# Reordering the start of a polynomial-interaction kernel: x on one queue, c1 ahead of D, low weights last

## What is computed

```python
for Wk, bk in zip(Ws, bs):
    z = jnp.einsum('bid,bjd->bdij', base, curr)
    curr = jnp.einsum('bdij,ijh->bhd', z, Wk) + bk[None, :, None]
    logit.append(curr)
pooled = jnp.sum(jnp.concatenate(logit, axis=1), axis=-1)
out = pooled @ lin_w + lin_b
```

## Time and profile before

| | us |
|---|---|
| median of 3 executions | 181.17 (180.68 to 181.23) |
| profiled execution, its own time | 181.1 |
| its span | 179.3 |
| TensorE busy | 173.2 (97%) |
| VectorE busy | 153.5 (86%) |
| ScalarE busy | 73.1 (41%) |
| GpSimd busy | 13.2 (7%) |

### The profile page before, as it was taken

The page is one execution under the profiler, slowest core; times in us unless marked ns, Lnnn a source line. Parts: engine busy times, 40 slices in busy tenths (PEclk is TensorE's granted clock), DMA queues, the critical chain, the costliest instruction groups (busy, mean ns, idle before and its releaser), DMA issues.

```text
span 179.3 us, 2565 instructions
## 1 busy us (share of the span) xinstructions
PE 173.2 (97%) x800; PEld 118.2 (66%) x800; DVE 153.5 (86%) x141; ACT 73.1 (41%) x80; POOL 13.2 (7%) x22
## 2 busy tenths in 40 slices
PE   6899987999999999999999999999999999999995
PEld 1273655777777777777777777777777777777762
DVE  0799976399999999999999999999999999994012
ACT  2556710064642464336432644264425542530020
POOL 3253904000000000000000000000000000000000
PEclk9999999999999999999999999999999999999999
DMA  5999744999878677857785779577947740000000
GB/s 165 396 411 399 263 103 121 419 413 412 280 237 301 158 230 230 325 133 236 229 302 163 228 228 310 162 224 236 327 134 227 229 149 0 0 0 4 0 0 0
DMA packets 12636, 37.59 MB, mean 210 GB/s; under 512 B 2548, under 2 KB 3668, under 8 KB 12628
## 3 DMA queue, kind: packets, MB, share of 16 engines
q1 hardware_dynamic: 11408, 36.39, 61.2%
q10 hardware_dynamic: 1156, 0.85, 1.8%
q0 software_dynamic: 64, 0.25, 0.4%
HBM read 36.40 MB, written 1.07 MB: 209 GB/s over the span
## 4 chain that ended last, share of the span: by engine, by line
PE 85%; DMA 6%; DVE 4%; SPq 2%; issue 1%; ACT 0%; DVEq 0%
PE q_ps L499 42%; PE c_ps L499 39%; DMA x_a<-xa 3%; DVE xb_z L263 2%; DMA pair_sb<-d_dram 2%; SPq L172 1%; DMA d_dram<-w_d 1%; PE q_ps L564 1%; PE q_ps L508 1%; PE c_ps L543 1%; SPq L166 1%; PE c_ps L638 1%; PE q_ps L543 1%; PE c_ps L642 0%; DVE acc L356 0%
## 5 line engine op out<-in xcount | busy, mean ns | idle before, releaser
L367 ACT ACTIVATE z_high<-xb_z 126x1024 fp32r<-126x1024 f32 x56 | 59.3, 1061 | 80.2 <-DVE xb_z L263 78.9
L270 DVE TENSOR_TENSOR z_low<-xb_z,z_high 126x1024 fp32r<-126x1024 f32 x56 | 69.2, 1241 | 0.5 <-ACT z_high L367 0.5
L263 DVE TENSOR_TENSOR xb_z<-x_a,xb_z 126x1024 f32<-126x1024 f32 x50 | 61.3, 1226 | 3.3 <-DMA xb_z<-xw 3.2
L499 PE MATMUL c_ps<-z_high,wc_high 126*101 126x512 f32 x112 | 35.3, 396 | 0.6 <-DVE z_low L270 0.6
L499 PE MATMUL c_ps<-z_low,wc_high 126*101 126x512 f32 x112 | 35.0, 394 | 0.0
L499 PE MATMUL c_ps<-z_high,wc_low 126*101 126x512 f32 x112 | 35.0, 393 | 0.0
L499 PE MATMUL q_ps<-z_high,wq_high 126*101 126x512 f32 x108 | 34.0, 396 | 0.9 <-DVE wq_low L313 0.9
L499 PE MATMUL q_ps<-z_high,wq_low 126*101 126x512 f32 x108 | 33.8, 394 | 0.0
L499 PE MATMUL q_ps<-z_low,wq_high 126*101 126x512 f32 x108 | 33.7, 393 | 0.0
L499 PEld LDWEIGHTS c_ps<-z_high,wc_high 126*101 126x101 f32 x112 | 18.3, 165 | 9.0 <-ACT z_high L367 1.1
L499 PEld LDWEIGHTS c_ps<-z_high,wc_low 126*101 126x101 f32 x112 | 18.5, 165 | 7.5
(11 more groups left out here) (59 smaller groups left out, 62.9 us busy)
## 6 DMA issues: line engine op xcount, KB each, us to landing
xb_z<-xw SPq DMA_DIRECT2D x50, 512.0 KB, 4.4
x_a<-xa SPq DMA_DIRECT2D x7, 512.0 KB, 4.8
w_post<-w1x SPq DMA_DIRECT2D x4, 512.0 KB, 8.7
w_d<-w2h SPq DMA_DIRECT2D x4, 404.0 KB, 6.4
pair_sb<-w_pairs SPq DMA_DIRECT2D x3, 202.0 KB, 9.9
xb_z<-xw ACTq DMA_DIRECT2D x2, 256.0 KB, 4.3
x_a<-xa SPq DMA_DIRECT2D x2, 256.0 KB, 4.5
d_dram<-w_d SPq DMA_DIRECT2D x2, 189.4 KB, 3.4
```

The source lines that it names most:

```text
L263: nc.vector.tensor_tensor(xb_z[0:K, c, :], x_a[0:K, u % 2, :], x_b, ALU.mult).then_inc(z_done, 1)
L270: nc.vector.tensor_tensor(z_low[0:K, m % SLOTS, :], xb_z[0:K, c, :], z_high[0:K, m % SLOTS, :].bitcast(fp32), ALU.subtract).then_inc(low_d ...
L367: nc.scalar.activation(z_high[0:K, m % SLOTS, :], xb_z[0:K, m % C, :], ACT.Copy).then_inc(high_done, 1)
L499: last = nc.tensor.matmul(ps[0:J, h * B:(h + 1) * B], w[0:K, c * J:(c + 1) * J], z[0:K, slot, h * B:(h + 1) * B], start=(c == 0 and k == 0 ...
```

## The change

1. The halves of x_b for chunk 0 are loaded from SyncE's queue, between those of x_a, no longer from ScalarE's.
2. Piece 1 of W0 is loaded ahead of W2.
3. In every chunk the pass with the weights' low part comes last (high x z_high, high x z_low, low x z_high), and each pass has its own wait: the first for the weights' high part and z_high, the second for z_low, the third for the weights' low part.
4. On TensorE chunk 0 of c1 stands ahead of all v pieces, chunk 1 between turn and D; selects 3 and 4 stand around the last v piece, select 5 behind D.
5. VectorE and ScalarE alternate forms, splits and roundings to fit; ScalarE casts piece 1 of W0 two roundings earlier.
6. The constant's matmul is among the c1 chunks (ahead of chunk 4) and its copy behind ScalarE's gathers.

```diff
             load_first_xa(0, xa_first)
+            load_first_xb(0, xb_first)
             load_first_xa(1, xa_loaded[0])
+            load_first_xb(1, xb_loaded[0])
             sp.dma_start(small_sb[:, :], small).then_inc(small_loaded, 16)
             load_w0(0)
+            load_w0(1)
             for i in range(VP):
                 load_w2(i)
-            load_w0(1)
...
             split(0, 1)
+            form(0, 3)
             split(0, 2)
-            form(0, 3)
             form(0, 4)
+            split(0, 3)
+            copy_d(2)
+            split(0, 4)
             form(0, 5)
-            copy_d(2)
-            split(0, 3)
             form(0, 6)
-            for m in range(4, C):
-                split(0, m)
+            split(0, 5)
+            split(0, 6)
...
             cast_w0(0)
             round_high(0, 1)
+            cast_w0(1)
             round_high(0, 2)
             act.wait_ge(v_multiplied, 1)
             nc.scalar.activation(v_rows[:, :], v_ps, ACT.Copy).then_inc(v_rows_copied, 1)
-            act.wait_ge(const_done, 1)
             act.wait_ge(v_turned, 1)
             nc.scalar.activation(v_sb[:, :], vt_ps, ACT.Copy).then_inc(v_copied, 1)
-            nc.scalar.activation(const_sb[:, :], const_ps, ACT.Identity, bias=linb,
-                                 scale=float(D)).then_inc(const_copied, 1)
-            cast_w0(1)
+            round_high(0, 3)
             copy_d(4)
             copy_d(0)
             copy_d(1)
-            round_high(0, 3)
+            round_high(0, 4)
             copy_d(3)
             cast_w0(2)
             cast_w0(3)
-            for m in range(4, BODY):
+            round_high(0, 5)
+            round_high(0, 6)
+            for m in range(C, BODY):
...
             def q_chunk(it, m):
                 u, c = divmod(m, C)
+                if m in PREP_CUTS[:2]:
+                    pe.wait_ge(wq_highs, PREP_CUTS.index(m) + 1)
+                if m == PREP_CUTS[2]:
+                    pe.wait_ge(last_highs, 1)
+                if c == 0:
+                    pe.wait_ge(q_psum_free, it * 2 + (u + 1))
+                chunk_pass(q_ps[u % 2], wq_high, z_high, m, True, False)
+                chunk_pass(q_ps[u % 2], wq_high, z_low, m, False, False)
                 if m in PREP_CUTS[:2]:
                     pe.wait_ge(wq_ready, PREP_CUTS.index(m) + 1)
                 if m == PREP_CUTS[2]:
                     pe.wait_ge(last_ready, 1)
-                if c == 0:
-                    pe.wait_ge(q_psum_free, it * 2 + (u + 1))
-                chunk_products(q_ps[u % 2], wq_high, wq_low, m).then_inc(z_slots_free, 1)
+                chunk_pass(q_ps[u % 2], wq_low, z_high, m, False, True).then_inc(z_slots_free, 1)
...
             select_xb(1)
             select_xb(2)
+            c1_chunk(0, 0)
             v_piece(0)
             v_piece(1)
-            c1_chunk(0, 0)
             v_piece(2)
+            select_xb(3)
             v_piece(3)
-            constant()
-            select_xb(3)
+            select_xb(4)
             turn_v()
-            select_xb(4)
+            c1_chunk(0, 1)
             d_group(4)
             d_group(0)
             d_group(1)
-            select_xb(5)
             d_group(2)
             d_group(3)
-            for m in range(1, C):
+            select_xb(5)
+            for m in range(2, C):
+                if m == PREP_CUTS[2]:
+                    pe.wait_ge(dgroup_copied_dve, 1)
+                    constant()
                 c1_chunk(0, m)
```

More of the change, by code:

```diff
@@ L185, in load_first_xa, with load_first_xb @@
                 sp.dma_start(x_a[:, 0, cols], xa[:, cols]).then_inc(loaded, 16)
+            def load_first_xb(h, loaded):
+                cols = slice(h * B, (h + 1) * B)
+                sp.dma_start(xb_z[:, 0, cols], xw[0:128, cols]).then_inc(loaded, 16)
             def load_xb(u, c):
@@ L387, in cast_w0 @@
                                      w0_sides[0:K, WC_CUTS[i]:WC_CUTS[i + 1], 0, :], ACT.Copy).then_inc(wc_highs, 1)
-            def load_first_xb(h, loaded):
-                cols = slice(h * B, (h + 1) * B)
-                act.dma_start(xb_z[:, 0, cols], xw[0:128, cols]).then_inc(loaded, 16)
             def round_xa(h, loaded):
@@ L396, in round_xa @@
                 nc.scalar.activation(x_split[0:K, cols], x_a[0:K, 0, cols], ACT.Copy).then_inc(xa_high, 1)
-            load_first_xb(0, xb_first)
-            load_first_xb(1, xb_loaded[0])
             round_xa(0, xa_first)
@@ L431, in _ @@
                 if m == C:
+                    act.wait_ge(const_done, 1)
+                    nc.scalar.activation(const_sb[:, :], const_ps, ACT.Identity, bias=linb,
+                                         scale=float(D)).then_inc(const_copied, 1)
+                    act.wait_ge(const_copied, 1)
                     act.wait_ge(z_done, C)
@@ L493, in _, with chunk_pass @@
         def _(pe):
-            def chunk_products(ps, high, low, m):
+            def chunk_pass(ps, w, z, m, first, last):
                 c, slot = m % C, m % SLOTS
[L497 to L502, removed]
+                for h in range(2):
+                    end = nc.tensor.matmul(ps[0:J, h * B:(h + 1) * B], w[0:K, c * J:(c + 1) * J],
+                                           z[0:K, slot, h * B:(h + 1) * B],
+                                           start=(c == 0 and first), stop=(c == C - 1 and last))
+                return end
             def last_q(m, cols):
                 c, slot = m % C, m % SLOTS
-                for k, (w, z) in enumerate(((wq_high, z_high), (wq_low, z_high), (wq_high, z_low))):
+                for k, (w, z) in enumerate(((wq_high, z_high), (wq_high, z_low), (wq_low, z_high))):
                     last = nc.tensor.matmul(q_ps[1][0:J, cols], w[0:K, c * J:(c + 1) * J], z[0:K, slot, cols],
@@ L514, in c1_chunk @@
                 if m in WC_CUTS[:-1]:
-                    pe.wait_ge(wc_ready, WC_CUTS.index(m) + 1)
+                    pe.wait_ge(wc_highs, WC_CUTS.index(m) + 1)
                 pe.wait_ge(high_done, it * BODY + (m + 1))
-                pe.wait_ge(low_done, it * BODY + (m + 1))
                 if c == 0 and u >= 1:
                     pe.wait_ge(c1_psum_free, it * 2 + (u + 1))
-                last = chunk_products(c1_ps[u % 2], wc_high, wc_low, m)
+                chunk_pass(c1_ps[u % 2], wc_high, z_high, m, True, False)
+                pe.wait_ge(low_done, it * BODY + (m + 1))
+                chunk_pass(c1_ps[u % 2], wc_high, z_low, m, False, False)
+                if m in WC_CUTS[:-1]:
+                    pe.wait_ge(wc_ready, WC_CUTS.index(m) + 1)
+                last = chunk_pass(c1_ps[u % 2], wc_low, z_high, m, False, True)
                 if c == C - 1:
@@ L580, in d_group @@
                     pe.wait_ge(v_copied, 1)
-                if place == 1:
-                    pe.wait_ge(const_copied, 1)
                 pe.wait_ge(w1_loaded[g], 16)
```

## The result

| us | before | changed |
|---|---|---|
| median | 180.66 (180.09 to 181.83, 19 executions) | 181.56 (180.61 to 183.85, 19 executions) |
| profiled execution, its own time | 181.1 | 183.52 |
| its span | 179.3 | 181.7 |

The ratio is 1.0047, with a 95% interval of 1.0033 to 1.0060: the change costs about 0.9 us, where the forecast was no change. 181.56 lies in the stated range, but by luck: the forecast was built on 181.17, the median of the first three executions of the kernel before, and the median of 19 is 180.66. Against that base the forecast was -0.06 us and the result is +0.9.

What follows compares the result with a forecast made beforehand. Bound: D's way through memory to the first q chunk, then a fixed 150.5 us on TensorE. Terms: x 0, stores +0.35, low part last -0.41, sum -0.06 us, so 181.1 us; range 180.2 to 182.1.

Steps and rivals of the forecast that it cites:

- The fixed part: TensorE from the first q chunk's start to the end: a fixed 150.5 us, so only the time before it matters.
- Halves of x on one queue: First loads of x: between -0.76 and +0.9 us possible, taken as 0 because the DMA engines are full.
- Rival 5: First loads: x halves late by their two issues, 0.9 us, all on the way to D: 182.0; chance 0.02.
- Chunk 1 of c1 ahead of D: On TensorE between turn and D: groups 0 and 1 1.3 us late, group 2 0.6, VectorE's copy 0.4.
- Stores: D's stores behind VectorE's copy: 0.35 of the copy's 0.4 us delay remains; last store landed at 23.9.
- Low part last: At q chunk 0: it needs only the weights' high part at first, so it starts earlier, -0.41 us.
- W0's piece: Early loads: W0's second piece comes at least 4 us earlier, W2's last piece 0.6 us later, hidden.
- rounding 6: On ScalarE ahead of its gathers: ends at 24.55, before 22.91; taken as 0 beyond SyncE's 0.35 us.
- c1's other waits: TensorE's later c1 chunks, waiting for VectorE's splits: c1 ends at about 27.5, below 28.4, hidden.
- Rivals 2 and 3: Slower ahead of q: ScalarE's gathers behind rounding 6 (181.9, chance 0.13); GpSimd's memset last (182.2, chance 0.08).
- Rival 4: On TensorE: each split wait breaks the matmul stream, 56 chunks by 0.09, 5 us: 186; chance 0.03.
- Rival 1: Faster: SyncE's full queue absorbs D's delay, x halves land up to 0.5 us earlier; -0.41 to -0.9: 180.4; chance 0.28.

Runs made afterwards that it cites:

- k9: The kernel before with the halves of x_b moved to SyncE's queue and nothing else: 182.11 us, ratio 1.0079 against before.
- k13: The changed kernel with 16 warm-up matmuls on TensorE instead of 14: 183.24 us, ratio 1.0119 against before.
- k3: The changed kernel with the halves of x_b back on ScalarE's queue: 181.15 us, ratio 1.0025 against before.
- k2: The changed kernel with c1's chunk 1 behind D instead of between turn and D: 181.42 us, ratio 1.0058 against before.
- k8: The changed kernel with x_b back on ScalarE's queue and c1's chunk 1 behind D: 180.44 us, ratio 0.9994 against before.
- k6: The changed kernel with eight unused warm-up matmuls keeping TensorE busy ahead of the first q chunk: 181.78 us, ratio 1.0071 against before.
- k4: The changed kernel with its 14 looped warm-up matmuls of 512 columns written out as 28 of 256: 181.36 us, ratio 1.0066 against before.
- k7: k1 with its 14 looped warm-up matmuls of 512 columns written out as 30 of 256: 180.51 us, ratio 0.9997 against before.
- k12: k8 with the two stores of D's group 3 issued by ScalarE instead of SyncE: 180.57 us, ratio 0.9997 against before.
- k11: k1 with the two stores of D's group 3 issued by ScalarE instead of SyncE: 180.18 us, ratio 0.9969 against before.
- k10: k8 with W0's second piece loaded behind W2 again: 182.39 us, ratio 1.0096 against before.
- k1: The kernel before with only the new order of passes and its split waits: 180.05 us, ratio 0.9976 against before.

## Why the prediction was wrong

*The fixed part held.* The time of the profiled execution less the start of q is 152.27 us before and 152.26 in k9 (the forecast's 150.5 is the same thing within the span, which is 1.8 shorter). In the ten profiles that have the new order of passes and no drop of the clock behind q it is 152.0 to 152.1. In the change and in k13, which have the drop, it is 153.7 and 153.4. So the result is set ahead of q, as the forecast put it, save for two things that it hadn't: the clock (1.4 to 1.6, in part of the executions), and some 0.2 that the order of passes gains behind q's start.

*"Halves of x on one queue … the engines are full … I take 0": this is the step that failed.* A DMA share of 1.04 showed them full with two queues. It doesn't follow that one queue fills them. k9 does this edit alone and is 1.2 to 1.4 slower; within the change it costs 0.4 (k3, intervals overlapping) to 1.0 (k2 against k8, apart). With one queue the first select came at 7.93, 8.31, 8.59, 8.90, 9.03 and 8.23 us (the change, k6, k13, k2, k4, k9); with two, at 7.83 to 8.04, save 8.54 in k7. It is a spread more than a shift, and the profiled execution of the change happens to stand at its good end: there the loads were slower (284 GB/s from 5 to 6 us) and the select wasn't. Late loads reach q in two ways: by the first select, and by W2, for which k9's v matmuls waited. Rival 5 had the place (0.02 of chance, 0.9 us), but only the two issues for a cause; the lower rate of the engines was in no rival. The Trainium skill (DMA: Bandwidth & Descriptors, Issuing engines are not separate DMA queues) says that several issuers save only the time of issuing. By it the loss would be two issues at most, 0.9 by the prediction's rows. k9's 1.2 to 1.4 is more, and its rate fell by a quarter, which issue time alone doesn't explain: here the measurement decides.

*Chunk 1 of c1 ahead of D: seen, and priced too low.* The forecast had groups 0 and 1 1.3 late, group 2 0.6, the copy 0.4, and 0.35 for the stores. Measured: turn 13.92 for 13.65, group 0 15.73 for 15.5, group 2 17.63 for 17.25, copy 18.73 for 18.35. Each is off by 0.2 to 0.4 in the same direction. By the runs the chunk costs 0.7 with two queues (k3 less k8) and 0.1 to 0.4 with one (the change less k2). In the change VectorE stood idle for 1.01 ahead of the copy, so TensorE held it. Without the chunk the copy comes at 17.38, right behind split 3 on VectorE: there VectorE's own order is the next bound, and it caps the gain.

*Stores: the runs don't price them.* I let the delay shrink (0.35 for 0.4). In the profile of the change it grew: from the end of the copy to the last landing it took 5.7 us (19.42 to 25.14), before 4.9 (18.65 to 23.56). This is the larger part of the miss in that profile, but not a part that the edit is shown to cause. k6 and k13 run the same program at this place, and took 4.9 and 6.5. Over the thirteen profiles that show the stretch it is 4.7 to 6.5, in no order by when the copy came: 6.0 and 6.2 where it was earliest (k8, k12), 4.8 in k11, 5.2 in k3 and k9, 5.8 in k2, 6.5 in k10, 4.7 where it was latest (k4). So neither my 0.05 of relief nor a growth can be read from one profile of each. The first issue behind the copy took 1.87, where before the longest took 1.21. What makes single issues long stays open: behind the copy they were 0.30 to 0.83 in k1, and the longest 1.60 in k13 and 1.42 in k10.

*Low part last: right.* -0.41 forecast; k1 gained 0.5, of which about 0.2 lies behind q's start, where the forecast had nothing.

*W0's piece, rounding 6, the constant, c1's other waits: hidden in the profile, as forecast.* Rounding 6 ended at 24.43 (24.55 forecast), the memset at 24.02 (23.8). Rivals 2 and 3 didn't decide, since the last store landed at 25.14. Rival 4 didn't come: without the clock's drop a chunk takes what it did, 0.23 a matmul (from 34.27 to 34.73 us for two).

*Rival 1* rested on the same row (1.21 against 0.46). Its half that x gains from one queue went the other way.

The sum by the runs, in medians: order of passes -0.5; the rest of the reorder without x and chunk 1 +0.4 (k8 less k1); chunk 1 ahead of D +0.7; one queue +0.4. Together +1.0, measured +0.9; the median of before differs by 0.1 between the comparisons. Taken in the other order, one queue first, the same runs give one queue +1.0 and chunk 1 +0.1. The +0.4 of k8 over k1 wasn't taken apart: their intervals overlap (0.9969 to 1.0019, 0.9962 to 0.9990), and what is behind it stays open.

## What to carry to other kernels

A DMA share of 1 measured with two issuing queues doesn't say that one queue would do the same: for the very first loads, on which everything waits, keep both, and test the edit alone. Work put ahead of a chain that runs through memory is paid at least in part: here a chunk of 1.39 us cost 0.7 in one pair of kernels and 0.1 in the other. One profile of each kernel can't price a burst of stores: the same program took 4.9 to 6.5 us for it. A change that moves six things is worth one run for each: here the one gain (-0.5) was hidden behind the losses, and alone it makes the faster kernel.

## What the runs showed of the hardware that was not expected

- The rate of the first loads: 272 to 293 GB/s in each microsecond from 3 to 7 us with all four halves of x on SyncE's queue (k9), 338 to 395 with two queues (before). As means of the four: 283 to 336 in the six profiles with one queue, 357 to 384 in the eight with two.
- TensorE's clock after an idle time: it fell to 0.50, for some 3 us, around the end of an idle time of 2.08 us (the change), 2.19 (k4, ahead of its first select) and 2.65 (k13), and not with 1.79, 1.69 and 1.60 (the profiles of k2, k3, k1). Executions with a mean clock of 0.991 were 2 of 19 in the change, 5 of 12 in k2, 3 of 10 in k4, 4 of 6 in k13, and 1 of 6 in k9 and none of 6 in k6, all with x on one queue. With x on two queues they were none of 60 in k1, k3, k7, k11 and k12, and 1 of 79 in the kernel before as it ran beside the experiments, but also 1 of 12 in k8 and 2 of 6 in k10. What makes TensorE wait for long can so cost twice: as a wait, and in some executions by the clock.
- An issue of a store on SyncE lasts from 0.30 (k1) to 1.87 us (the change), and the last store lands 2.0 to 4.8 us after the last issue (k12 the longest).
